# First attention of a two-layer decoder block: scores on four row quarters of the array

## The chip, the core and the metric

One core of a Trainium2 chip. The metric is device time of one execution in microseconds (us); lower is better. The engines are named as in the profile: PE is TensorE (matmuls; PEld its weight loads), DVE is VectorE, ACT is ScalarE, POOL is GpSimd, SP the queue that issues transfers.

## What is computed

Two layers, each an attention over a latent context and a feed-forward block, on x of 32 x 100 x 256. The change touches the attention of the first layer alone:

```python
x = x + tanh(g_xattn[0]) * _L0_xattn_ref(layernorm(x), ctx_512, Wq, Wkv_expand, Wout)

def _L0_xattn_ref(q, latent_kv, Wq, Wkv_expand, Wout):      # 16 heads of 16
    qp = q @ Wq.T
    k, v = jnp.split(latent_kv @ Wkv_expand.T, 2, axis=-1)
    scores = einsum('bhqd,bhkd->bhqk', qh, kh) / sqrt(16)
    scores = where(causal, scores, finfo.min)
    out = einsum('bhqk,bhkd->bhqd', softmax(scores), vh)
    return out @ Wout.T
```

The mask is causal, so of the 1444 context rows only the first 100 matter to 100 query rows, and the kernel loads only these.

## The kernel before

The program runs one phase after another: loading, first attention, experts, second attention, second feed-forward. `phase_l0_attention` (line 79) is the phase that changes. It takes the 32 batch elements ("batches" below) in 8 groups of 4, and its engines each run a list of instructions in the order in which the code is written, with semaphores between them; there is no scheduler. A group first makes its dense products on PE (`dense`, nine steps: normalised rows and latents transposed, queries at line 360, keys at 366, values at 372), which DVE copies out (`evacuate`). Queries and keys then lie with the 256 head dimensions on partitions, in two chunks k of 128, so 8 heads of 16 partitions in each chunk; `qt` and `kt` hold 100 columns a batch.

For each batch, 16 heads go in four quarters q of 4 heads, each with a bank of the accumulation memory, `s_ps[:, q]`, 4 x 100 columns:

- DVE (`block_keys`, line 222): the keys of a batch, repeated 8 times along the columns and multiplied by a selector, so that each head's columns are zero outside its own 16 partitions. That is `kbd`, 128 x 800 for each chunk.
- PE (`scores`): a bfloat16 matmul writes the mask into the bank (383), then one float32 matmul of 128 rows and 400 columns adds the scores of four heads (384). The float32 matmul stands in the trace as two.
- DVE (`differences`): maximum over each head's keys (234) and scores minus maximum (238). ACT takes the exponential (323).
- PE transposes the four heads' probabilities (425), ACT copies them (316), PE multiplies them with the values, which carry a column of ones (414). With four quarters done DVE divides by the sums (245, 247), PE transposes the result (394) and projects it (400), and DVE adds it to x (252).

The order around the change is written out by hand in PE's `group`: scores of batch 0, and then, in batch b and quarter q, first the scores of batch b + 1 and quarter q, then the transposes of batch b and quarter q, then the values of quarter q - 1. In the last batch of a group the dense steps of the next group stand between. DVE's list is in step: in batch b and quarter q it handles the differences of batch b + 1 and quarter q, and between them `block_keys`, `add_x` and the next group's row statistics. The bank of a quarter is free for new scores when DVE has taken the differences of the batch before; that is the wait on `diff_ready`:

```python
pe.wait_ge(diff_ready, PRIMED + n - NQ + 1 if b > 0 else it * G * NQ)
o = s_ps[0:S, q, 0:4 * S]
pe.matmul(o, identb[0:S, 0:S], mask[:]..., start=True, stop=False)
mm = pe.matmul(o, qt[:, q // 2, b * S:(b + 1) * S], kbd[b % 2][:, q // 2, 4 * (q % 2):4 * (q % 2) + 4, :]..., start=False, stop=True)
```

Of the kernel before, what the change touches and what calls it, by code (L numbers as in the profile page):

```python
# [9 lines left out]
ALU = mybir.AluOpType  # L10
# [3 lines left out]
B, S, D = 32, 100, 256  # L14
LK, DL = 1444, 64
G = 4
NG = B // G
T = G * S
KT = D // 128
H = 16  # L20
HD = D // H
# [13 lines left out]
PRIMED = 1  # L35
# [43 lines left out]
def phase_l0_attention(nc, outer, sem, io, m):  # L79

    NQ = 4
    counters = []
    with ExitStack() as ctx:
        sb = lambda n, s, d=F32: ctx.enter_context(nc.sbuf_tensor(n, s, d))
# [11 lines left out]
        mask_raw = sb("a_mask_raw", [S, S])  # L96
        mask = sb("a_mask", [S, 4, S], BF16)
        identb = sb("a_identb", [128, 128], BF16)
        headsel_raw, headsel = sb("a_headsel_raw", [128, 8]), sb("a_headsel", [128, 8, S])
        latg = sb("a_latg", [S, G + 1, DL])  # L100
        stats, mv, ve, rstd = sb("a_stats", [S, G, 6]), sb("a_mv", [S, G, 2]), sb("a_ve", [S, G]), sb("a_rstd", [S, G])
        xn = sb("a_xn", [S, G, D])
# [1 line left out]
        latt = [sb(f"a_latt{i}", [DL, T], F32R) for i in range(2)]  # L104
        qt = sb("a_qt", [128, KT, T])
        kt = sb("a_kt", [128, KT, T])
        kbd = [sb(f"a_kbd{i}", [128, KT, 8, S]) for i in range(2)]
        va = sb("a_va", [S, G, H, HD + 1])
        mx = sb("a_mx", [S, NQ, 4])
        diff = sb("a_diff", [S, NQ, 4, S])  # L110
# [1 line left out]
        pt = sb("a_pt", [S, 2, 4, S])  # L112
# [3 lines left out]
        s_ps = ps("a_s_ps", [128, 4, 512])  # L116
        p_ps = ps("a_p_ps", [128, 2, 512])
        o_ps = ps("a_o_ps", [128, 512])
        f_ps = ps("a_f_ps", [128, 512])
        w_loaded, w_ready = sem("a_w_loaded"), count("a_w_ready")  # L120
# [3 lines left out]
        kbd_ready, split_hi, latg_ready = count("a_kbd_ready"), count("a_split_hi"), count("a_latg_ready")  # L124
# [10 lines left out]
        with nc.Block() as block:  # L135
# [36 lines left out]
            def _(v):  # L172
# [7 lines left out]
                v.memset(va[:, :, :, HD], 1.0).then_inc(w_ready, 1)  # L180
                v.memset(latg[:, G, :], 0.0).then_inc(w_ready, 1)
                v.tensor_copy(identb[:], m.ident[:]).then_inc(w_ready, 1)
                v.tensor_copy(headsel[:], headsel_raw[:].unsqueeze(2).broadcast_to((128, 8, S))).then_inc(w_ready, 1)
                v.wait_ge(w_ready, PRIMED + NW)
                def row_stats(it):
                    xg = lambda j: m.x[:, bass.ds((it * G + j) * D, D)]
# [29 lines left out]
                def block_keys(it, b):  # L216

                    if b >= 2:

                        v.wait_ge(s_ready, PRIMED + (it * G + b - 1) * NQ)  # L220
                    for k in range(KT):
                        ins = v.tensor_tensor(kbd[b % 2][:, k], headsel[:],
                                              kt[:, k, b * S:(b + 1) * S].unsqueeze(1).broadcast_to((128, 8, S)),
                                              ALU.mult)
                    ins.then_inc(kbd_ready, 1)

                def group(it, more):
                    xg = lambda j: m.x[:, bass.ds((it * G + j) * D, D)]
# [103 lines left out]
            def _(pe):  # L332
# [41 lines left out]
                    mm.then_inc(dense_mm, 1)  # L374

                def group(it, more):
                    def scores(b, q):
                        n = it * G * NQ + b * NQ + q
                        pe.wait_ge(kbd_ready, PRIMED + it * G + b + 1)

                        pe.wait_ge(diff_ready, PRIMED + n - NQ + 1 if b > 0 else it * G * NQ)
                        o = s_ps[0:S, q, 0:4 * S]
                        pe.matmul(o, identb[0:S, 0:S], mask[:].rearrange("p h k -> p (h k)"), start=True, stop=False)
                        mm = pe.matmul(o, qt[:, q // 2, b * S:(b + 1) * S],
                                       kbd[b % 2][:, q // 2, 4 * (q % 2):4 * (q % 2) + 4, :].rearrange("p h k -> p (h k)"),
                                       start=False, stop=True)
                        mm.then_inc(s_ready, 1)

                    def turn_out(b):
                        nb = it * G + b  # L390
                        pe.wait_ge(cn_ready, PRIMED + nb + 1)
                        pe.wait_ge(x_added, PRIMED + nb)
                        for k in range(KT):
                            mm = pe.transpose(f_ps[:, 256 + k * S:256 + (k + 1) * S], cn[:, k * 128:(k + 1) * 128], m.ident[0:S, 0:S])
                        mm.then_inc(ct_ready, 1)

                    def project_out(b):
                        pe.wait_ge(ct_copied, PRIMED + it * G + b + 1)
                        for k in range(KT):
                            mm = pe.matmul(f_ps[0:S, 0:D], ct[:, k, :], wo[:, k, :], start=(k == 0), stop=(k == KT - 1))  # L400
                        mm.then_inc(f_ready, 1)
                    pe.wait_ge(dense_out, PRIMED + (it + 1) * ND)
                    for q in range(NQ):
                        scores(0, q)
                    for b in range(G):
                        nb = it * G + b

                        def probs_value(q):
                            n = nb * NQ + q
                            pe.wait_ge(pt_copied, PRIMED + n + 1)  # L410
                            if q == 0:
                                pe.wait_ge(cn_ready, PRIMED + nb)
                            for h in range(4):
                                mm = pe.matmul(o_ps[0:S, (4 * q + h) * (HD + 1):(4 * q + h + 1) * (HD + 1)],
                                               pt[:, q % 2, h, :], va[:, b, 4 * q + h, :], start=True, stop=True)
                            mm.then_inc(pv_done, 1)
                        for q in range(NQ):
                            n = nb * NQ + q
                            if b + 1 < G:
                                scores(b + 1, q)  # L420
                            pe.wait_ge(prob_ready, PRIMED + n + 1)
                            if b * NQ + q >= 2:
                                pe.wait_ge(pt_copied, PRIMED + n - 1)
                            for h in range(4):
                                mm = pe.transpose(p_ps[0:S, q % 2, h * S:(h + 1) * S], prob[:, q, h, :], m.ident[0:S, 0:S])
                            mm.then_inc(pt_ready, 1)
                            if q == 0 and b > 0:
                                turn_out(b - 1)
                            if q == 2 and b > 0:
                                project_out(b - 1)  # L430
                            if b == G - 1 and more:
                                for k in BESIDE_MM[q]:
                                    dense(it + 1, k)
                            if q > 0:
                                probs_value(q - 1)
                        probs_value(NQ - 1)
                    if more:
                        for k in range(7, ND):
                            dense(it + 1, k)
                    turn_out(G - 1)  # L440
                    project_out(G - 1)
# [1423 lines left out]
def constants():  # L1865
    import numpy as np
    c = {}
    c["ident"] = np.eye(128, dtype=np.float32)
    q, k = np.arange(S)[:, None], np.arange(S)[None, :]
    c["causal"] = np.where(k <= q, 0.0, -1e30).astype(np.float32)  # L1870
    c["headsel"] = (np.arange(128)[:, None] // HD == np.arange(8)[None, :]).astype(np.float32)
    row_expert = np.arange(E * I) // I
    rows = np.zeros((40, E * I), np.float32)
    for e in range(E):
# [50 lines left out]
```

## Time and profile before

| what | value |
|---|---|
| time, median of 3 runs | 3704.04 us (3701.6 to 3706.81) |
| time of the profiled execution | 3701.05 us |
| its span, first to last instruction | 3699.2 us |
| PE busy | 3111.9 us, 84% of the span |
| DVE busy | 2443.3 us, 66% |
| mean granted clock of PE | 0.924 |
| first attention, from its first score matmul to its end | 41.7 to 445.7 us |

The profile is of one execution. Its rows give start and length of instructions or groups of them; lengths of PE's matmuls contain a modelled end that lies under the next one, so what one occupies is read from start to start. PEclk is the granted share of PE's clock: 1.00 is 2.4 GHz, 0.50 is 1.2 GHz.

### The profile page before, as it was taken

What the parts mean: (1) busy time and instruction counts of PE and PEld (TensorE: products, weight loads), DVE (VectorE), ACT (ScalarE), POOL (GpSimd) and SP (SyncE); (2) the same over time, 40 slices, a digit from 0 to 9 for tenths busy, and PEclk for the clock granted to TensorE, in tenths of its full rate; (3) what the DMA queues carried; (4) which work ended last, traced back from release to release, by engine and by line L of the source; (5) the groups of instructions that cost most, each with busy time, mean ns of one, the idle gap of its engine ahead of it and who ended that gap; (6) DMA issues with size and microseconds to landing.
All of it is one profiled execution on the core that took longest, in us unless ns stands there. A gap on an engine that the chain in (4) does not pass through costs nothing. (4 is left out here: it accounts for less than half of the span.)

```text
span 3699.2 us, 56177 instructions
## 1 busy us (share of the span) xinstructions
PE 3111.9 (84%) x16648; PEld 2139.2 (58%) x16656; DVE 2443.3 (66%) x3485; ACT 1282.0 (35%) x2714; POOL 1581.2 (43%) x1062
## 2 busy tenths in 40 slices
PE   6999799997789988989888998898988899888244
PEld 5777688886555555555555555555555555555123
DVE  5777744443666676676676666667667667764787
ACT  1333222221243333333333333333332343333356
POOL 0000022221455545545555554554555555554467
PEclk9899799998899999999999999999999999999566
DMA  3000000002100000000000000000000000000200
GB/s 100 0 0 0 23 20 0 0 0 76 27 18 16 16 13 18 16 6 23 18 10 19 16 16 13 18 16 6 23 19 9 19 16 16 7 14 11 78 13 23
DMA packets 129494, 70.05 MB, mean 19 GB/s; under 512 B 83497, under 2 KB 123785, under 8 KB 129155
## 3 DMA queue, kind: packets, MB, share of 16 engines
q1 hardware_dynamic: 129218, 66.79, 7.2%
q8 instruction: 123, 2.02, 0.2%
q14 instruction: 153, 1.25, 0.1%
HBM read 56.30 MB, written 10.04 MB: 18 GB/s over the span
## 5 line engine op out<-in xcount | busy, mean ns | idle before, releaser
L1079 POOL TENSOR_TENSOR c_psum<-c_p 120x800 f32<-120x800 f32 (+1 forms) x384 | 758.8, 1976 | 873.4 <-ACT c_p L1291 492.9
L1136 DVE TENSOR_REDUCE c_mneg<-c_m_ps 128x1 fp32r<-128x1452 f32 (+1 forms) x448 | 746.5, 1666 | 440.2 <-PE c_m_ps L1330 433.6
L1291 ACT ACTIVATE c_p<-c_s_ps 120x400 f32<-120x400 f32 (+1 forms) x1536 | 650.0, 510 | 957.2 <-PE c_s_ps L1413 886.2
L1426 PE MATMUL c_o_ps<-c_p,c_val 120*64 120x400 f32 (+1 forms) x3072 | 609.8, 519 | 0.0
L1412 PE MATMUL c_s_ps<-c_q,c_k 128*120 128x400 f32 (+1 forms) x1536 | 556.4, 362 | 37.1 <-DMA c_q<-c_mneg 28.9
L1413 PE MATMUL c_s_ps<-c_q,c_k 65*120 65x400 f32 (+1 forms) x1536 | 539.6, 351 | 0.0
L1330 PE MATMUL c_m_ps<-c_k,c_q 128*128 128x484 f32 (+1 forms) x1344 | 408.4, 412 | 95.6 <-DVE c_mneg L1136 94.7
L1330 PEld LDWEIGHTS c_m_ps<-c_k,c_q 128*128 128x128 f32 (+1 forms) x1344 | 211.2, 179 | 329.9 <-DVE c_mneg L1136 215.2
L1070 POOL TENSOR_TENSOR c_rot<-c_rc,c_rs 96x400 f32<-96x400 f32 x256 | 261.3, 1040 | 281.0 <-DVE c_rs L1178 279.5
L1412 PEld LDWEIGHTS c_s_ps<-c_q,c_k 128*120 128x120 f32 (+1 forms) x1536 | 287.2, 187 | 128.4 <-issue 108.1
L1426 PEld LDWEIGHTS c_o_ps<-c_p,c_val 120*64 120x64 f32 (+1 forms) x3072 | 189.4, 138 | 271.1 <-issue 154.0
L1159 DVE TENSOR_TENSOR c_acc<-c_acc,c_psum 120x800 f32<-120x800 f32 x256 | 317.7, 1241 | 23.5 <-POOL c_psum L1079 21.1
L1353 PE MATMUL c_s_ps<-c_xt,l_a 128*96 128x400 f32 x1536 | 307.1, 351 | 1.8 <-DVE c_xt L1124 1.8
L1413 PEld LDWEIGHTS c_s_ps<-c_q,c_k 65*120 65x120 f32 (+1 forms) x1536 | 287.6, 187 | 12.7
L1353 PEld LDWEIGHTS c_s_ps<-c_xt,l_a 128*96 128x96 f32 x1536 | 248.0, 164 | 58.9 <-issue 11.6
L1247 ACT ACTIVATE c_q<-c_o_ps 64x400 fp32r<-64x400 f32 x256 | 127.7, 499 | 398.4 <-PE c_o_ps L1368 393.7
L522 POOL TENSOR_TENSOR b_act_lo<-b_act,b_act_hi 128x400 fp32r<-128x400 f32 x88 | 91.6, 1045 | 322.6 <-ACT b_act_hi L664 322.6
L709 PE MATMUL b_gu_ps<-b_xt,l_a 128*128 128x400 f32 x1056 | 213.9, 354 | 11.2 <-DVE b_gated L556 11.2
L709 PEld LDWEIGHTS b_gu_ps<-b_xt,l_a 128*128 128x128 f32 x1056 | 193.4, 193 | 18.1 <-DVE b_gated L556 18.0
L1343 PE MATMUL c_m_ps<-l_cvo,c_ct 128*100 128x256 f32 x512 | 132.6, 418 | 52.3 <-DVE c_ct L1144 45.7
L1178 DVE TENSOR_TENSOR c_rc<-c_s_ps,c_qcos 96x400 f32<-96x400 f32 x256 | 144.5, 565 | 33.2 <-PE c_s_ps L1353 27.5
L1144 DVE TENSOR_TENSOR c_ct<-c_onum,c_rdb 128x400 f32<-128x400 f32 x64 | 111.7, 1745 | 61.1 <-DMA c_rdb<-l_denominators 60.9
(218 smaller groups left out, 4159.7 us busy)
## 6 DMA issues: line engine op xcount, KB each, us to landing
c_rdb<-l_denominators SPq DMA_DIRECT2D x128, 100.0 KB, 2.7
c_kv<-in_ctx SPq DMA_DIRECT2D x32, 360.0 KB
c_q<-c_mneg SPq DMA_DIRECT2D x384, 0.5 KB, 1.9
c_den<-c_oden SPq DMA_DIRECT2D x256, 0.8 KB
x_rows<-in_x SPq DMA_DIRECT2D x4, 800.0 KB
x_spill<-x_rows SPq DMA_DIRECT2D x1, 3200.0 KB
c_xa<-x_spill SPq DMA_DIRECT2D x8, 400.0 KB
c_xr<-x_spill SPq DMA_DIRECT2D x32, 100.0 KB
```

Source lines behind the costliest of these rows:

```text
L709: mm = pe.matmul(gu_ps[:, t % 2, j, 0:T], w[wi][:, k, t * 128:(t + 1) * 128], xt[x][:, k, :], start=(i == 0 and k == 0), stop=(i == 2 and ...
L1070: g.tensor_tensor(rot[:, i % 4, a, :], rc[:, a, :], rs[:, a, :], ALU.add).then_inc(rot_ready, 1)
L1079: g.tensor_tensor(psum[0:k, u % 2, :], p[0:k, 2 * u % 4, :], p[0:k, (2 * u + 1) % 4, :], ALU.add).then_inc(psum_ready, 1)
L1136: v.tensor_reduce(mneg[0:n, c, t:t + 1], m_ps[0:n, :, 0:4 * KP], AX.XY, ALU.max, negate=True).then_inc(mneg_ready, 1)
L1159: v.tensor_tensor(acc[0:k, :], acc[0:k, :], psum[0:k, q % 2, :], ALU.add).then_inc(acc_ready, 1)
L1178: v.tensor_tensor(dst[:, a, :].rearrange("p (b s) -> p b s", b=G), wide_bank(i, half)[0:HALF, 0:T].rearrange("p (b s) -> p b s", b=G), tab ...
L1291: a.activation(p[0:k, w % 4, i * HALFQ:(i + 1) * HALFQ], s_ps[0:k, (2 * w + i) % 4, 0:HALFQ], ACT.Exp).then_inc(exp_ready, 1)
L1330: mm = pe.matmul(m_ps[0:n, k, 0:4 * KP], q1[:, j, c * CQS + t * 128:c * CQS + t * 128 + n], k1[j % 2][:, k * 4 * KP:(k + 1) * 4 * KP], sta ...
L1353: mm = pe.matmul(wide_bank(i, a)[0:HALF, 0:T], m.a[w][:, k, HEADS[i], a * HALF:(a + 1) * HALF], xt[x][:, k, :], start=(q == 0 and k == 0), ...
L1412: pe.matmul(o, k1[j % 2][:, r * KP:r * KP + k], q1[:, j, cols], start=True, stop=False)
L1413: mm = pe.matmul(o, k2[j % 2][:, r * KP:r * KP + k], q2[:, j, cols], start=False, stop=True)
L1426: mm = pe.matmul(o_ps[i * DL:(i + 1) * DL, 0:HALFQ], val[0:k, j % 2, r, :], p[0:k, w % 4, i * HALFQ:(i + 1) * HALFQ], start=(r == 0), stop ...
```

## The change

The 16 heads are grouped anew, and the scores of a batch are written as one block. Partitions 32q to 32q + 31 of each chunk hold two heads. Quarter q now takes these two heads of chunk 0 and the two of chunk 1 (table `QH`), so each of its matmuls reads 32 partitions alone: two heads, 200 columns. `kbd` needs only two head slots a chunk (selector of 2 columns in place of 8, repeating every 32 partitions), made by one DVE instruction of 128 x 400. `scores(b)` writes four masks into four banks, then eight matmuls, chunk by chunk and in each chunk quarter by quarter, on rows 0, 32, 64 and 96 in turn. It stands once ahead of a batch's loop over quarters, no longer inside it.

```diff
+    QH = [(2 * q, 2 * q + 1, H // 2 + 2 * q, H // 2 + 2 * q + 1) for q in range(NQ)]
...
-        kbd = [sb(f"a_kbd{i}", [128, KT, 8, S]) for i in range(2)]
+        kbd = [sb(f"a_kbd{i}", [128, KT, 2, S]) for i in range(2)]
...
-                    for k in range(KT):
-                        ins = v.tensor_tensor(kbd[b % 2][:, k], headsel[:],
-                                              kt[:, k, b * S:(b + 1) * S].unsqueeze(1).broadcast_to((128, 8, S)),
-                                              ALU.mult)
-                    ins.then_inc(kbd_ready, 1)
+                    v.tensor_tensor(kbd[b % 2][:], headsel[:].unsqueeze(1).broadcast_to((128, KT, 2, S)),
+                                    kt[:, :, b * S:(b + 1) * S].unsqueeze(2).broadcast_to((128, KT, 2, S)), ALU.mult).then_inc(kbd_ready, 1)
...
-                    def scores(b, q):
-                        n = it * G * NQ + b * NQ + q
+                    def scores(b):
+                        n = it * G * NQ + b * NQ
                         pe.wait_ge(kbd_ready, PRIMED + it * G + b + 1)
-
-                        pe.wait_ge(diff_ready, PRIMED + n - NQ + 1 if b > 0 else it * G * NQ)
-                        o = s_ps[0:S, q, 0:4 * S]
-                        pe.matmul(o, identb[0:S, 0:S], mask[:].rearrange("p h k -> p (h k)"), start=True, stop=False)
-                        mm = pe.matmul(o, qt[:, q // 2, b * S:(b + 1) * S],
-                                       kbd[b % 2][:, q // 2, 4 * (q % 2):4 * (q % 2) + 4, :].rearrange("p h k -> p (h k)"),
-                                       start=False, stop=True)
-                        mm.then_inc(s_ready, 1)
+                        for q in range(NQ):
+                            pe.wait_ge(diff_ready, PRIMED + n - NQ + q + 1 if b > 0 else it * G * NQ)
+                            pe.matmul(s_ps[0:S, q, 0:4 * S], identb[0:S, 0:S], mask[:].rearrange("p h k -> p (h k)"), start=True, stop=True)
+                        for k in range(KT):
+                            for q in range(NQ):
+                                rows = slice(32 * q, 32 * q + 32)
+                                mm = pe.matmul(s_ps[0:S, q, 2 * k * S:2 * (k + 1) * S], qt[rows, k, b * S:(b + 1) * S],
+                                               kbd[b % 2][rows, k].rearrange("p h k -> p (h k)"), start=False, stop=True, skip_group_check=True)
+                                if k == KT - 1:
+                                    mm.then_inc(s_ready, 1)
...
-                    for q in range(NQ):
-                        scores(0, q)
+                    scores(0)
...
-                                mm = pe.matmul(o_ps[0:S, (4 * q + h) * (HD + 1):(4 * q + h + 1) * (HD + 1)],
-                                               pt[:, q % 2, h, :], va[:, b, 4 * q + h, :], start=True, stop=True)
+                                mm = pe.matmul(o_ps[0:S, QH[q][h] * (HD + 1):(QH[q][h] + 1) * (HD + 1)],
+                                               pt[:, q % 2, h, :], va[:, b, QH[q][h], :], start=True, stop=True)
                             mm.then_inc(pv_done, 1)
+                        if b + 1 < G:
+                            scores(b + 1)
                         for q in range(NQ):
                             n = nb * NQ + q
-                            if b + 1 < G:
-                                scores(b + 1, q)
```

PE, batch 0 of a group, behind the scores of batch 0, as it stands before (each REGISTER_ALU forms the value that the next instruction waits for):

```order
L383 MATMUL a_s_ps<-a_mask,a_identb 100x400
L384 MATMUL a_s_ps<-a_kbd,a_qt 100x400
L425 MATMUL a_p_ps<-ident,a_prob 100x100 x4
L381 REGISTER_ALU
L383 MATMUL a_s_ps<-a_mask,a_identb 100x400
L384 MATMUL a_s_ps<-a_kbd,a_qt 100x400
L425 MATMUL a_p_ps<-ident,a_prob 100x100 x4
L412 REGISTER_ALU
L414 MATMUL a_o_ps<-a_va,a_pt 100x17 x4
```

One mask and one score matmul of batch 1 stand ahead of each four transposes of batch 0. The same place in the changed kernel:

```order
L380 MATMUL a_s_ps<-a_mask,a_identb 100x400
L379 REGISTER_ALU
L380 MATMUL a_s_ps<-a_mask,a_identb 100x400
L384 MATMUL a_s_ps<-a_kbd,a_qt 100x200 x8
L424 MATMUL a_p_ps<-ident,a_prob 100x100 x8
L411 REGISTER_ALU
L413 MATMUL a_o_ps<-a_va,a_pt 100x17 x4
```

These are the last two of the four masks; all four, each with its own wait on `diff_ready`, and the eight score matmuls of batch 1 have moved ahead of the first transpose of batch 0.

DVE at the start of a group, before:

```order
L222 TENSOR_TENSOR a_kbd<-a_headsel,a_kt 128x800 x2
L232 ISA
L234 TENSOR_REDUCE a_mx<-a_s_ps 100x4
L238 TENSOR_TENSOR a_diff<-a_s_ps,a_mx 100x400
L232 REGISTER_ALU
```

and in the changed kernel:

```order
L222 TENSOR_TENSOR a_kbd<-a_headsel,a_kt 128x400
L230 ISA
L232 TENSOR_REDUCE a_mx<-a_s_ps 100x4
L236 TENSOR_TENSOR a_diff<-a_s_ps,a_mx 100x400
L230 REGISTER_ALU
```

Here only the key selection differs: one instruction of half the columns for two; DVE's order stays.

## Rows read from the trace of the kernel before

**Rows 1.** The page, part 1: busy time of each engine over the span.
```profile
PE 3111.9 (84%) x16648; PEld 2139.2 (58%) x16656; DVE 2443.3 (66%) x3485; ACT 1282.0 (35%) x2714; POOL 1581.2 (43%) x1062
```
**Rows 2.** Stretches of the stage: length, busy time (instructions) by engine, PEclk, DMA share, GB/s.
```profile
41.70:445.70 404.00, 373.94 (x2406) 291.57 (x2406) 307.56 (x607) 131.27 (x288) 9.45 (x13) 0.87 0.01 4
128.00:134.00 6.00, 6.00 (x24) 5.42 (x24) 1.60 (x4) 0.50 (x1) 0.00 (x0) 0.50 0.00 0
135.00:138.00 3.00, 3.00 (x26) 2.58 (x24) 1.49 (x3) 0.50 (x1) 0.00 (x0) 1.00 0.00 0
139.00:147.00 8.00, 7.57 (x26) 5.46 (x26) 4.08 (x10) 0.34 (x1) 0.40 (x1) 0.50 0.00 0
149.00:178.00 29.00, 27.64 (x207) 21.17 (x206) 26.00 (x57) 13.53 (x30) 1.01 (x1) 1.00 0.00 0
428.80:435.00 6.20, 6.20 (x34) 5.66 (x33) 3.29 (x3) 1.72 (x4) 0.00 (x0) 0.50 0.00 0
```
**Rows 3.** Timeline of PE, one quarter at 2.4 GHz: start us, length us, instruction.
```profile
204.54 0.35 PE L383 MATMUL a_s_ps<-a_mask,a_identb 100*100 100x400 bf16 x1
204.73 0.84 PE L384 MATMUL a_s_ps<-a_kbd,a_qt 128*100 128x400 f32 x2
205.41 0.51 PE L425 MATMUL a_p_ps<-ident,a_prob 100*100 100x100 f32 x4
205.75 0.80 PE L414 MATMUL a_o_ps<-a_va,a_pt 100*100 100x17 f32 x8
206.40 0.35 PE L383 MATMUL a_s_ps<-a_mask,a_identb 100*100 100x400 bf16 x1
```
**Rows 4.** Timeline of PE in the stretches at 1.2 GHz.
```profile
127.75 2.18 PE L360 MATMUL a_s_ps<-a_xt,a_wq 128*128 128x400 f32 x6 [1.34 <-DVE a_xt L205]
129.73 1.40 PE L414 MATMUL a_o_ps<-a_va,a_pt 100*100 100x17 f32 x8
130.97 0.89 PE L425 MATMUL a_p_ps<-ident,a_prob 100*100 100x100 f32 x4
131.65 1.92 PE L400 MATMUL a_f_ps<-l_cvo,a_ct 128*100 128x256 f32 x4
...
139.69 2.88 PE L372 MATMUL a_s_ps<-a_wv,a_latt 64*100 64x256 f32 x12
142.50 0.59 PE L394 MATMUL a_f_ps<-ident,a_cn 100*128 100x100 f32 x2
143.52 2.03 PE L400 MATMUL a_f_ps<-l_cvo,a_ct 128*100 128x256 f32 x4 [0.43 <-ACT a_ct L309]
145.34 0.54 PE L383 MATMUL a_s_ps<-a_mask,a_identb 100*100 100x400 bf16 x1
145.67 1.54 PE L384 MATMUL a_s_ps<-a_kbd,a_qt 128*100 128x400 f32 x2
147.01 0.54 PE L383 MATMUL a_s_ps<-a_mask,a_identb 100*100 100x400 bf16 x1
```
**Rows 5.** Key matmuls on 64 rows: timeline of PE, and line 366 (ns min/median/max).
```profile
84.79 0.53 PE L425 MATMUL a_p_ps<-ident,a_prob 100*100 100x100 f32 x4
85.25 1.36 PE L366 MATMUL a_s_ps<-a_latt,a_wk 64*128 64x400 f32 x6
...
L366 PE MATMUL a_s_ps<-a_latt,a_wk x48: 338/342/450, 36.2 to 390.1; 64*128 64x400 f32 x48
```
**Rows 6.** Timeline of DVE: reduces of a group's start, and a key selection.
```profile
199.73 0.57 DVE L234 TENSOR_REDUCE a_mx<-a_s_ps 100x4 f32<-100x400 f32 x1
...
200.82 0.56 DVE L234 TENSOR_REDUCE a_mx<-a_s_ps 100x4 f32<-100x400 f32 x1
...
206.27 1.88 DVE L222 TENSOR_TENSOR a_kbd<-a_headsel,a_kt 128x800 f32<-128x800 f32 x2
208.07 0.57 DVE L234 TENSOR_REDUCE a_mx<-a_s_ps 100x4 f32<-100x400 f32 x1
```
**Rows 7.** Timeline of PE: the first transposes of the same group.
```profile
202.36 0.51 PE L425 MATMUL a_p_ps<-ident,a_prob 100*100 100x100 f32 x4
```

More of the change, by code:

```diff
@@ L98, in phase_l0_attention @@
         identb = sb("a_identb", [128, 128], BF16)
-        headsel_raw, headsel = sb("a_headsel_raw", [128, 8]), sb("a_headsel", [128, 8, S])
+        headsel_raw, headsel = sb("a_headsel_raw", [128, 2]), sb("a_headsel", [128, 2, S])
         latg = sb("a_latg", [S, G + 1, DL])
@@ L182, in _ @@
                 v.tensor_copy(identb[:], m.ident[:]).then_inc(w_ready, 1)
-                v.tensor_copy(headsel[:], headsel_raw[:].unsqueeze(2).broadcast_to((128, 8, S))).then_inc(w_ready, 1)
+                v.tensor_copy(headsel[:], headsel_raw[:].unsqueeze(2).broadcast_to((128, 2, S))).then_inc(w_ready, 1)
                 v.wait_ge(w_ready, PRIMED + NW)
@@ L1870, in constants @@
     c["causal"] = np.where(k <= q, 0.0, -1e30).astype(np.float32)
-    c["headsel"] = (np.arange(128)[:, None] // HD == np.arange(8)[None, :]).astype(np.float32)
+    c["headsel"] = (np.arange(128)[:, None] // HD % 2 == np.arange(2)[None, :]).astype(np.float32)
     row_expert = np.arange(E * I) // I
```

## The prediction

> **What bounds the kernel now.** I read the page first, then the stage, then one quarter of a batch, then the clock. The page names TensorE (PE) as the busiest engine, 84% of the span [rows 1]. The stage that the change touches runs from 41.7 to 445.7 us: 404 us for eight groups of four batches, 50.5 us a group; PE is busy for 374 us of it and VectorE (DVE) for 308 [rows 2]. So PE sets the pace, and DVE is not far behind. One quarter of a batch at 2.4 GHz takes 1.86 us on PE without a gap: mask 0.19, score pair 0.68, four transposes 0.34, probabilities times values 0.65 [rows 3]. The "x2" on the score matmul is one float32 matmul run as two passes over the same rows of the array.
>
> The third thing to read is the clock. In the whole stage it stands at 0.87, so at 1.2 GHz for about a quarter of the time [rows 2]. What the engine did before it moved: from 149 to 178 us, with score pairs all along, it stands at 1.00. From 128 to 134 us PE is busy without a break (query weights, transposes, values) and the clock is 0.50. It rises to 1.00 for 135 to 138, right behind the query-weight matmuls, which are 128 rows high and 400 columns long; in that stretch PE is again busy without a break, with key matmuls 64 rows high and short value products, and then the clock falls and stays at 0.50 from 139 to 147, until masks and score pairs come. From 428.8 to 435, after the last score pair, PE is fully busy at 0.50 [rows 2, 4]. So "busy" on the page did not go with the high clock. What went with it, in these stretches or just ahead of them, were long matmuls of full height, and in a regular batch those are above all the four score pairs.
>
> **The change, part by part.** All is summed against the profiled execution's own 3701.05 us (span 3699.2, 1.85 around it); the median of the runs shown, 3704.04, is 3 us above it.
>
> *Score matmuls.* Removed: four pairs a batch, 4 x 0.68 = 2.72 us [rows 3]. Added: eight matmuls of 200 columns on 32 rows, each two passes, and each half a pair long, 0.34 us. No row of this trace has matmuls on different rows side by side, so the bounds are one after the other, 8 x 0.34 = 2.72 us (nothing gained), and four quarters abreast, 0.68 us plus the tail. I take 1.5 us: the two passes of one matmul need the same rows, so with starts in program order, as in every row here, only the second pass of one quarter and the first of the next can run together, 8 x 0.17, and 0.17 behind it. Sixteen weight loads instead of eight cost nothing more: the eight loads and short matmuls of a value product pass in 0.65 us [rows 3], so sixteen need 1.3 us, beside the 1.5.
>
> *Switching the array's height.* The key matmuls on 64 rows behind full-height transposes start at 85.25, where 84.79 + 0.34 = 85.13 was free, 0.12 late, and the longest of them takes 450 ns against a median of 342, 0.11 more [rows 5]; with another 0.12 for the way back I take 0.35 us for a switch there and back, once a batch, 32 x 0.35 = 11 us (lower end 0.11 x 32 = 4).
>
> *Masks.* The same four a batch, 0.19 us each: nothing. *Selected keys on DVE.* Two instructions of 800 elements, 1.80 us from start to start, become one of 400; a reduce over 400 takes 0.57 [rows 6]. That frees 1.3 us a batch on an engine that PE hides; I count zero. If DVE became the bound it would be worth up to 32 x 1.3 = 42 us. The values' head order changes only addresses. The smaller load and copy of the selector lie in the start, under the input load: below 1 us.
>
> *The moved order.* Today the transposes of batch 0 start at 202.36, 2.6 us after the first reduce at 199.73, when one quarter's difference is through [rows 6, 7]. Now scores of batch 1 stand ahead of them as a block, and its last mask needs all four differences of batch 0, at 1.09 us each [rows 6]. PE then waits at each group's start for 4 x 1.09 less three or four masks, 3.6 us; behind it are queued the transposes, and behind those ACT's copies. That is 8 x 3.6 = 29 us. In the other batches the differences are finished beside transposes and value products; a wait of about 1 us where DVE also has the next group's statistics I leave in the range.
>
> *At an unchanged clock* this gives -32 x (2.72 - 1.5) + 11 + 29 = +1 us: 3702.
>
> *The clock.* The score matmuls now cover 32 rows instead of 128 and a shorter time, as the key matmuls on 64 rows cover half. After their stretch the clock fell [rows 2], and now nothing but masks and the output projection is both long and nearly full in height. I forecast 1.2 GHz for most of the stage. Its price from rows at 0.50 [rows 4], for one batch: masks 4 x 0.33 (145.34 to 145.67) = 1.3; scores, half a pair of 1.34 (145.67 to 147.01) is 0.67, two abreast 0.335, 8 x 0.335 + 0.335 = 3.0; transposes 4 x 0.68 (130.97 to 131.65) = 2.7; value products 4 x 1.24 (129.73 to 130.97) = 5.0; projection 1.8 (143.52 to 145.34); turning the output 0.4 (of 0.59 with its tail); switches 0.35. Sum 14.6 us, four batches 58.4. The dense work of a group: twelve transposes at 0.17 (a quarter of 0.68), 2.0; query weights 2 x 1.98 (127.75 to 129.73), 4.0; keys, 1.36 at the high clock [rows 5], 2.6; values 2.8 (139.69 to 142.50): 11.4. Waits: the group's start 3.4, before the query weights 1.34, before the projection 0.43: 5.2. Together 75.0 us a group. In between the clock will rise behind the query weights as it did at 135, for some 3 us and at times twice; what runs there would have taken double, so I take off 5: 70.0. Against 50.5 that is +19.5 a group, 8 x 19.5 = +156 us, 3857. With three high stretches a group it is 65, 3817; with none 75, 3897.
>
> **Rivals.** *1. A busy PE keeps its clock.* Then the sum above holds, 3702, within the bound of what a measurement of this kernel can tell from no change, 0.2% or 7.4 us. For it: PE stays busy for most of the stage. Against it: 128 to 134 and 428.8 to 435, busy to the last tenth and at 0.50 [rows 2]. The Trainium skill, "TensorE: Matmul & The Clock Gate", section "Why this matters for your kernels", has it that a TensorE kept busy without long gaps between bursts keeps the high clock; by that rule the time is this rival's 3702, and these two stretches disagree with it.
>
> *2. The quarters run fully abreast and the clock holds* (the side of faster). Mechanism: the array takes one pass of each quarter at a time, so a batch's scores take 0.68 + 0.17 = 0.85 us instead of 1.5, 32 x 0.65 = 21 us less: 3681. It decides as soon as scores fall below about 1.3 us a batch and the stage's clock is 0.87 or better. Against it: two passes on the same rows, and the clock. The same page, section "Measured speedup vs the span model", measured 3.07 times for four row quarters; a batch's scores would by that be an estimated 0.89 us. No run here shows it. At the low clock this case comes to 32 x 1.3 = 42 us less than the forecast, 3815, and belongs to it.
>
> *3. The quarters do not overlap at all, at the low clock*: 8 x 0.67 = 5.4 instead of 3.0 us a batch, 32 x 2.4 = 77 us more: 3934. For it: nothing in this trace shows two matmuls side by side.
>
> *4. The clock falls only behind the new wait at the group's start.* Then one stretch of 3 to 6 us a group at half speed costs 1.7 to 3.4 us: 3702 + 14 to 27, 3716 to 3729. For it: long waits of PE are the other thing that stands ahead of falls (1.34 us idle just before 127.75 [rows 4]). Against it: falls that no wait precedes.
>
> **How the numbers follow.** Forecast (mostly low clock, quarters two or four abreast) 0.66; rival 1, 0.06; rival 2, 0.10; rival 3, 0.08; rival 4, 0.10. The predicted time is the forecast's 3857; its own range is 3815 to 3897. The range 3700 to 3900 takes in rivals 1 and 4 and leaves out 2 and 3, together 0.18. Slower is forecast, 3 and 4: 0.84; same is 1: 0.06; faster is 2: 0.10.
>
> **What would show it.** Right: clock of the stage near 0.55, a group of 65 to 75 us, value products of 1.24 us a quarter nearly everywhere, key selection at 0.57 us, PE idle about 3.5 us at a group's start with single masks in it. The eight score matmuls of a batch in 1.5 us (3.0 at the low clock) confirm two abreast; 0.9 or 2.7 (1.7 or 5.4) refute it. The prediction is wrong if the stage's clock stays at 0.8 or more: then the time is near 3700 and its sign hangs on the width of the overlap.

## The result, and the profile after

The changed kernel takes 3788.28 us (median of 4 runs, 3778.96 to 3798.03) against 3705.43 us for the kernel before on the same chip: a ratio of 1.0227, 95% interval 1.0205 to 1.025. It is slower, by 83 us. The profiled execution took 3778.96 us, its span is 3777.2.

The page, part 1:

```profile
PE 3171.6 (84%) x16904; PEld 2207.9 (58%) x16912; DVE 2403.6 (64%) x3453; ACT 1278.2 (34%) x2714; POOL 1582.5 (42%) x1062
```

The key selection on DVE, by line (count, ns min/median/max, first and last start, shape):

```profile
L222 DVE TENSOR_TENSOR a_kbd<-a_headsel,a_kt x32: 562/565/576, 41.0 to 489.2; 128x400 f32<-128x400 f32 x32
```

PE's share is the same 84% as in [rows 1], though its score matmuls became shorter. The stage, and four stretches in it (columns as in [rows 2]):

```profile
41.70:519.30 477.60, 433.34 (x2662) 357.59 (x2662) 269.98 (x576) 126.47 (x288) 9.46 (x13) 0.63 0.01 4
106.50:111.00 4.50, 2.01 (x20) 0.96 (x19) 3.95 (x8) 1.07 (x2) 0.00 (x0) 0.87 0.00 0
112.50:125.00 12.50, 12.50 (x85) 10.47 (x84) 5.48 (x11) 3.60 (x8) 0.00 (x0) 0.50 0.00 0
127.00:132.80 5.80, 5.01 (x49) 4.34 (x47) 5.51 (x17) 3.02 (x7) 1.01 (x1) 1.00 0.00 0
134.00:145.00 11.00, 10.95 (x62) 9.84 (x58) 6.77 (x15) 3.85 (x10) 0.00 (x0) 0.50 0.00 0
```

The stage grew from 404.0 to 477.6 us, 73.6 of the 78.0 us by which the span grew (3699.2 to 3777.2). Its clock fell from 0.87 [rows 2] to 0.63. Between two levels, 0.63 means that 2 x (1 - 0.63) = 74% of the stage, 353 us, ran at 1.2 GHz; before it was 26%, 105 us. From 112.5 to 125 us PE is busy without any break and stands at 0.50 throughout.

What happens there, in PE's timeline (start us, length us, instruction, in brackets the idle time before it):

```profile
106.56 0.94 PE L384 MATMUL a_s_ps<-a_kbd,a_qt 32*100 32x200 f32 x16
108.75 0.37 PE L380 MATMUL a_s_ps<-a_mask,a_identb 100*100 100x400 bf16 x1 [1.25 <-DVE a_diff L236]
109.84 0.57 PE L380 MATMUL a_s_ps<-a_mask,a_identb 100*100 100x400 bf16 x1 [0.71 <-DVE a_diff L236]
110.93 0.57 PE L380 MATMUL a_s_ps<-a_mask,a_identb 100*100 100x400 bf16 x1 [0.52 <-DVE a_diff L236]
112.02 0.57 PE L380 MATMUL a_s_ps<-a_mask,a_identb 100*100 100x400 bf16 x1 [0.51 <-DVE a_diff L236]
112.52 1.67 PE L384 MATMUL a_s_ps<-a_kbd,a_qt 32*100 32x200 f32 x16
114.12 1.57 PE L424 MATMUL a_p_ps<-ident,a_prob 100*100 100x100 f32 x8
115.69 1.51 PE L413 MATMUL a_o_ps<-a_va,a_pt 100*100 100x17 f32 x8
...
197.22 0.37 PE L380 MATMUL a_s_ps<-a_mask,a_identb 100*100 100x400 bf16 x1 [0.60 <-DVE a_diff L236]
197.52 0.94 PE L384 MATMUL a_s_ps<-a_kbd,a_qt 32*100 32x200 f32 x16
198.39 0.55 PE L424 MATMUL a_p_ps<-ident,a_prob 100*100 100x100 f32 x4
```

This shows both things that the prediction priced. The four masks of batch 1 at a group's start come singly, each waiting for DVE. And the sixteen passes of a batch's scores take 198.39 - 197.52 = 0.87 us at 2.4 GHz where four pairs took 2.72 [rows 3], and 114.12 - 112.52 = 1.60 us at 1.2 GHz. So the matmuls themselves are three times as fast as before, and the stage is longer all the same. The 0.87 from 106.5 to 111 us says where the clock fell: at 109.8, inside this wait. By the trace's clock records it fell inside the wait at the start in seven of the eight groups (in the first it was low already).

PE's waits in the stage (us in total, times, longest), after, and then before:

```profile
PE a_s_ps L380 <- DVE a_diff L236: 28.3, 37, 1.3
PE a_f_ps L394 <- DVE a_cn L245: 8.8, 5, 6.1
PE a_s_ps L358 <- DVE a_xt L206: 2.5, 7, 0.4
```

```profile
PE a_f_ps L394 <- DVE a_cn L247: 18.8, 23, 6.1
PE a_s_ps L360 <- DVE a_xt L205: 6.5, 7, 1.3
```

The new wait on the differences is 28.3 us, but 10.0 and 4.0 us of other waits have gone: PE comes to them later. The account is then, with low-clock time counted at half: before, 404 - 105/2 = 351 us of full-speed time; after, 477.6 - 353/2 = 301. The change takes 50 us away, and the clock takes 353/2 - 105/2 = 124 us, which makes the +74. (It is rough, since a wait for DVE does not shrink with PE's clock. Counting only the time in which PE was busy at 1.2 GHz, 92.9 us before and 335.5 after by the trace's clock records, the clock takes 121 us, the waits 14, and the work itself is 62 us less.)

### The profile page after: what moved, and what is told of

Its sections match the earlier page's. It is cut to its first block and busy times, and to the rows that moved or that the text cites. A ratio compares the mean times of both kernels' runs of the same rounds, so it can differ in the third digit from the quotient of the medians.

```text
span 3777.2 us, 56624 instructions
## 1 busy us (share of the span) xinstructions
PE 3171.6 (84%) x16904; PEld 2207.9 (58%) x16912; DVE 2403.6 (64%) x3453; ACT 1278.2 (34%) x2714; POOL 1582.5 (42%) x1062
## 5 line engine op out<-in xcount | busy, mean ns | idle before, releaser
L1135 DVE TENSOR_REDUCE c_mneg<-c_m_ps 128x1 fp32r<-128x1452 f32 (+1 forms) x448 | 746.4, 1666 | 439.3 <-PE c_m_ps L1329 432.8
L413 PEld LDWEIGHTS a_o_ps<-a_va,a_pt 100*100 100x100 f32 x1024 | 151.9, 239 | 10.1 <-issue 4.7
```

Source lines behind the costliest of these rows:

```text
L413: mm = pe.matmul(o_ps[0:S, QH[q][h] * (HD + 1):(QH[q][h] + 1) * (HD + 1)], pt[:, q % 2, h, :], va[:, b, QH[q][h], :], start=True, stop=True)
L1135: v.tensor_reduce(mneg[0:n, c, t:t + 1], m_ps[0:n, :, 0:4 * KP], AX.XY, ALU.max, negate=True).then_inc(mneg_ready, 1)
```

## Experiments

Two theories stood at the start. A: score matmuls of 32 rows no longer hold the clock. B: it is the idle time at the group's start, which the moved order brings, that lets it fall. All runs of the kernel before beside them had medians from 3696.8 to 3704.7 us. Stage and clock are those of each run's one profiled execution.

| run | median us | ratio to before (95%) | stage us | clock of stage |
|---|---|---|---|---|
| before (profile) | 3704.0 | | 404.0 | 0.87 |
| changed | 3788.3 | 1.0227 (1.0205 to 1.025) | 477.6 | 0.63 |
| e1_order_alone | 3737.2 | 1.0096 (1.0058 to 1.0134) | 432.8 | 0.85 |
| e2_rows_alone | 3964.2 | 1.0694 (1.0662 to 1.0726) | 652.6 | 0.53 |
| e3_fill_every_batch | 3744.4 | 1.0115 (1.0083 to 1.0147) | 430.1 | 0.88 |
| e4_fill_start | 3751.4 | 1.0137 (1.0101 to 1.0173) | 453.1 | 0.69 |
| e5_late_block | 3834.8 | 1.036 (1.0321 to 1.0398) | 527.7 | 0.57 |
| e6_late_block_fill | 3864.0 | 1.0438 (1.0398 to 1.0478) | 571.1 | 0.72 |
| e7_late_block_half_fill | 3829.4 | 1.0353 (1.0301 to 1.0405) | 527.7 | 0.73 |
| e8_late_block_mask_twice | 3835.8 | 1.0365 (1.0326 to 1.0404) | 526.2 | 0.66 |
| e9_fill_mid | 3749.6 | 1.0138 (1.0093 to 1.0182) | 451.7 | 0.71 |
| e10_half_fill | 3787.4 | 1.0226 (1.0188 to 1.0265) | 485.3 | 0.70 |
| e11_mask_twice | 3800.5 | 1.026 (1.0216 to 1.0303) | 503.5 | 0.63 |
| e12_fill_odd | 3720.9 | 1.005 (1.0033 to 1.0067) | 427.5 | 0.79 |

### The two halves of the change apart

Order alone: the block of four masks and scores, each score matmul on 128 rows and 400 columns as before, and the key selection as before too. The diffs here and below are against the changed kernel, shortened.

```diff
-                        for k in range(KT):
-                            for q in range(NQ):
-                                mm = pe.matmul(... qt[rows, k, ...], kbd[b % 2][rows, k]...)
+                        for q in range(NQ):
+                            mm = pe.matmul(s_ps[0:S, q, 0:4 * S], qt[:, q // 2, ...], kbd[b % 2][:, q // 2, 4 * (q % 2):4 * (q % 2) + 4, :]...)
```

> The moved order alone: the score matmuls as before (128 rows, 400 columns, key selection of 800 columns), but the four masks and four score matmuls of a batch stand as one block ahead of the transposes, as in the changed kernel. Theory A (the 32-row score matmuls no longer keep PE's clock up): the granted clock of the first attention stays at 0.80 or more, PE waits some 3.5 us at each group's start, and the time is 3725 to 3765 us. Theory B (the wait at the group's start is what drops the clock): the clock of the stage falls to 0.70 or less as in the changed kernel, and the time is above 3790 us, since the scores are also four times as long.

Rows alone: 32-row score matmuls, in the order of the kernel before, one quarter's mask and four passes ahead of each four transposes.

```diff
-                    def scores(b):
+                    def scores(b, q):
...
-                        for k in range(KT):
-                            for q in range(NQ):
+                        rows = slice(32 * q, 32 * q + 32)
+                        for k in range(KT):
...
+                            if b + 1 < G:
+                                scores(b + 1, q)
```

> The 32-row score matmuls alone: key selection of 400 columns, two heads on 32 partitions, but the quarters in the order of the kernel before (mask and two score matmuls of one quarter of the next batch ahead of each four transposes), so no quarter runs beside another and PE has no wait at a group's start. Theory A: the clock of the stage falls to 0.55 to 0.65 and the time is 3830 to 3890 us. Theory B: the clock stays at 0.85 or more; only four switches of the array's height a batch are added, 32 x 4 x 0.35 = 45 us: 3735 to 3755 us.

The order alone costs 35 us and keeps 0.85. PE's wait on the differences in it:

```profile
PE a_s_ps L382 <- DVE a_diff L238: 15.2, 23, 0.7
```

That is half of the changed kernel's 28.3 us, so this run tests B with half of the idle time. The rows alone cost 262 us and bring 0.53. The whole stage and a stretch of the second, its longest waits of PE in the stage, and one quarter in its timeline:

```profile
40.80:693.40 652.60, 639.30 (x2662) 484.98 (x2662) 280.29 (x576) 129.63 (x288) 9.47 (x13) 0.53 0.01 5
60.00:690.00 630.00, 617.69 (x2590) 471.31 (x2590) 270.98 (x559) 125.86 (x280) 9.47 (x13) 0.53 0.00 0
```

```profile
PE a_f_ps L391 <- DVE a_cn L245: 6.1, 1, 6.1
PE a_f_ps L397 <- ACT a_ct L307: 3.4, 8, 0.4
```

```profile
300.50 0.55 PE L379 MATMUL a_s_ps<-a_mask,a_identb 100*100 100x400 bf16 x1
300.98 1.65 PE L382 MATMUL a_s_ps<-a_kbd,a_qt 32*100 32x200 f32 x4
302.56 0.91 PE L422 MATMUL a_p_ps<-ident,a_prob 100*100 100x100 f32 x4
```

There is no wait on the differences at all, PE is busy for 617.69 of 630 us, and the clock is at its low level nearly all the time. So the low clock does not need B's idle time, and rival 1 is refuted. It also parts two things that the prediction named together, 32 rows and a shorter time: here a quarter's mask and scores take longer than before, and the clock is lower still. What the wait adds in the changed kernel, where the clock falls inside it, is left to the next runs. The Trainium skill, "TensorE: Matmul & The Clock Gate", section "Why this matters for your kernels", advises to keep TensorE busy continuously for the high clock; the stretch from 60 to 690 us, busy for 98% and at 0.53, is the plainest disagreement in the case. The time lies 74 us above theory A's upper end. Of these, 50 are explained by a lone quarter, which overlaps with nothing: mask to first score 0.48 us and four passes with their way back 1.58, together 2.06, where mask and pair at 1.2 GHz took 1.67 before [rows 4]; 128 x 0.39 = 50 us.

### Putting full-height work back

A matmul whose result the mask overwrites, ahead of every mask (e3, the diff shown), and under `if b == 1:` ahead of the masks of batch 1 alone, inside the waits of a group's start (e4).

```diff
+                            pe.matmul(s_ps[0:S, q, 0:D], wo[:, 0, 0:S], wo[:, 0, :], start=True, stop=True)
                             pe.matmul(s_ps[0:S, q, 0:4 * S], identb[0:S, 0:S], mask[:]..., start=True, stop=True)
```

> The changed kernel with work added: ahead of every mask one float32 matmul of 128 rows and 256 columns on the output weights, written to the same bank and overwritten by the mask; the output is unchanged. That adds four times 0.43 us a batch at 2.4 GHz, 55 us in all. Theory A: the clock of the stage rises to 0.80 or more, and in spite of the added work the time falls below the changed kernel's 3788 us, to 3690 to 3740. Theory B: only the filler in the group's start wait helps; then this comes out some 30 to 50 us above e4.

> The changed kernel with the same added matmul, but only ahead of the four masks of batch 1 of each group, where PE waits for DVE anyway, so that the wait is filled with full-height work. Theory A: the clock of the stage stays between 0.60 and 0.70 and the time within 15 us of 3788. Theory B: the clock goes back to 0.85 and the time to 3690 to 3715 us.

The stage with the filling in every batch, and two instructions of it:

```profile
40.70:470.80 430.10, 385.21 (x2917) 306.35 (x2915) 268.70 (x575) 125.14 (x288) 9.45 (x13) 0.88 0.02 6
```

```profile
202.88 0.60 PE L380 MATMUL a_s_ps<-l_cvo 128*100 128x256 f32 x2
203.32 0.33 PE L381 MATMUL a_s_ps<-a_mask,a_identb 100*100 100x400 bf16 x1
```

Each filling takes 203.32 - 202.88 = 0.44 us, so 128 x 0.44 = 56 us of useless work were added, and the kernel became 44 us faster than the changed one; the clock is back at 0.88. This is theory A's strongest support: no operand or order of the changed kernel differs but for this work, and PE's idle time in the stage is the same (430.10 - 385.21 = 44.9 us against 477.60 - 433.34 = 44.3). The filling at the start alone also helped, by 37 us, more than A had allowed. Two readings were left: it fills idle time (then idle time is a second cause, called C below), or its amount helps wherever it stands. The same dose in batch 3, where PE hardly waits (3.4 of the 28.3 us), tells them apart.

```diff
+                            if b == 3:
+                                pe.matmul(s_ps[0:S, q, 0:D], wo[:, 0, 0:S], wo[:, 0, :], start=True, stop=True)
```

> The changed kernel with one matmul of full height (128 rows, 256 columns, two passes, 0.43 us at 2.4 GHz, overwritten by the mask) ahead of each of the four masks of batch 3 alone, where PE has hardly a wait: 4 a group, 32 in all, 14 us of work at 2.4 GHz, the same dose that at the group's start, inside the waits, gave a clock of 0.69 and 3751 us. Theory A (the amount of full-height work counts, wherever it stands): clock 0.67 to 0.73, 3745 to 3780 us. Theory C (what the filling did there was to fill idle time, and idle time is a second cause of falls): clock 0.60 to 0.65, 3790 to 3815 us, which is the changed kernel's time plus 14 to 28.

3749.6 us at 0.71, the same as at the start: C falls. The stages of e4 and e9 say the same, with 37.5 and 49.8 us of idle time against the changed kernel's 44.3:

```profile
41.00:494.10 453.10, 415.57 (x2726) 338.59 (x2726) 270.18 (x576) 126.21 (x288) 9.46 (x13) 0.69 0.01 5
```

```profile
40.30:492.00 451.70, 401.87 (x2726) 324.78 (x2726) 269.38 (x576) 125.72 (x288) 9.46 (x13) 0.71 0.02 6
```

PE's timeline and three stretches around one such place in e9:

```profile
122.40 0.65 PE L381 MATMUL a_s_ps<-l_cvo 128*100 128x256 f32 x2
122.89 0.34 PE L382 MATMUL a_s_ps<-a_mask,a_identb 100*100 100x400 bf16 x1
...
124.97 0.94 PE L386 MATMUL a_s_ps<-a_kbd,a_qt 32*100 32x200 f32 x16
```

```profile
103.60:117.00 13.40, 13.40 (x89) 11.10 (x89) 6.02 (x12) 3.60 (x8) 0.00 (x0) 0.50 0.00 0
118.00:132.00 14.00, 13.89 (x132) 11.87 (x130) 12.09 (x32) 6.81 (x17) 1.01 (x1) 1.00 0.00 0
134.00:144.00 10.00, 8.66 (x70) 7.82 (x68) 6.13 (x12) 1.93 (x4) 0.00 (x0) 1.00 0.00 0
```

The start of this group is untouched: it waits as in the changed kernel, then 13 us at 0.50. The clock rises just ahead of the filling, as in the changed kernel at 127; but there it fell again at the next block of scores (0.50 from 134), and here, with the filling, it holds through that block to 144.

### The same block, moved later

> The changed kernel with the block of batch b + 1's masks and scores moved later in PE's list: ahead of the transposes of quarter 3 in a group's batch 0, of quarter 2 in batch 1, of quarter 1 in batch 2 (in the change: ahead of quarter 0 in each). The work is the same; PE has batch 0's first transposes and value products to do while DVE finishes its differences, so the idle time at a group's start (about 3.5 us) should go. Theory A (score matmuls on 32 rows no longer hold the clock): clock of the stage stays at 0.55 to 0.68, and the time falls by no more than the 29 us of waits, 3755 to 3790 us. Theory B (the idle time at the group's start lets the clock fall): clock 0.80 or more, and the stage is that of before less 32 x (2.72 - 0.87) = 59 us for the scores, 3640 to 3690 us. Both at work, as the run with filling at the start alone suggested: clock 0.68 to 0.80, 3690 to 3755 us.

```diff
-                        if b + 1 < G:
-                            scores(b + 1)
                         for q in range(NQ):
                             n = nb * NQ + q
+                            if b + 1 < G and q == 3 - b:
+                                scores(b + 1)
```

With the same later block, the filling as in e3, half of it, and each mask written twice:

> The kernel with the later block, and with one more matmul of full height ahead of every mask (128 rows, 256 columns, two passes, 0.43 us at 2.4 GHz, its result overwritten by the mask): 16 a group, 128 x 0.43 = 55 us of added work. Theory A: clock of the stage 0.85 or more; against the run with this filling at the change's own place (3744 us) the waits go, up to 29 us, so 3710 to 3740 us. Theory B: the clock is that of the run without filling, and the time is its time plus 55 us or more.

> As the run with the later block and filling, but with 128 columns in place of 256: 128 x 0.22 = 28 us of added work. Theory A, if half of it still holds the clock: 0.85 or more, 3685 to 3715 us; if it doesn't, the clock lies between those of the two other runs with the later block, 3715 to 3760 us. Theory B: the time of the run without filling plus 28 us.

> The kernel with the later block, each mask written twice (a bfloat16 matmul of 100 rows and 400 columns, 0.17 to 0.19 us at 2.4 GHz), so 128 x 0.18 = 23 us of added work that changes no result. Theory A, if one bfloat16 pass counts as much as a float32 pass of the same length: like the half filling, clock and time within 0.05 and 20 us of that run. If bfloat16 does not count, the clock is that of the run without filling and the time that run's plus 23 to 45 us. Theory B: the time of the run without filling plus 23 us at its clock.

Of theory A's bounds e5 missed the upper by 45 us, e6 by 124 and e7 by 69; e8 came within 20 us of e7, as expected, but 0.07 below its clock. Theory B missed as well: it had 3640 to 3690 us for e5. The waits of PE in e5's stage, and the stages of e5 and e8:

```profile
PE a_f_ps L394 <- DVE a_cn L245: 38.4, 18, 6.1
PE a_p_ps L424 <- ACT a_prob L321: 17.5, 16, 1.8
```

```profile
40.20:567.90 527.70, 464.66 (x2662) 383.20 (x2662) 269.26 (x576) 131.72 (x288) 9.46 (x13) 0.57 0.01 5
```

```profile
41.00:567.20 526.20, 444.00 (x2790) 356.15 (x2790) 268.81 (x577) 131.62 (x288) 9.46 (x13) 0.66 0.02 6
```

The 28.3 us on the differences are gone, and 38.4 + 17.5 took their place. The 17.5 stand at the groups' starts, two waits in each: PE now waits there for ACT's exponentials. The 38.4 had not been followed: DVE's list divides by the sums (line 245) only behind the differences of the next batch. A later block makes these late, and PE's turn of the output, next in PE's own list, waits for the division, 18 times in the stage. Of the 50 us by which e5's stage is longer than the changed kernel's, 19 are idle time (527.70 - 464.66 = 63.0 against 44.3 us); the rest is busy time, at a lower clock. So the block's early place, wait included, is the cheaper one.

Between A and B, e5 decides little: the idle time at a group's start shrank, from 3.1 to 2.2 us, but did not go, and other waits had come. What the four runs show is that added work raised the clock here too, the doubled masks included (0.66 in e8 against 0.57 in e5), and that it gained no time clear of noise, since PE's idle time grew with it (82.2 us in e8, 101.5 in e6).

### How much work, and how spread

The changed kernel's own order, with half the filling (128 columns) at every mask; with each mask written twice; and with the full filling in batches 1 and 3.

```diff
+                            pe.matmul(s_ps[0:S, q, 0:128], wo[:, 0, 0:S], wo[:, 0, 0:128], start=True, stop=True)
...
+                            pe.matmul(s_ps[0:S, q, 0:4 * S], identb[0:S, 0:S], mask[:]..., start=True, stop=True)
...
+                            if b % 2 == 1:
+                                pe.matmul(s_ps[0:S, q, 0:D], wo[:, 0, 0:S], wo[:, 0, :], start=True, stop=True)
```

> The changed kernel, its order kept, with a full-height matmul of 128 columns (0.22 us at 2.4 GHz) ahead of every mask: 128 x 0.22 = 28 us of work, half of the run in which 256 columns gave a clock of 0.88 and 3744 us. Theory A: if half is enough, clock 0.80 or more and 3705 to 3740 us (3744 less up to 28, some of which the waits already hid); if not, clock 0.68 to 0.80 and 3735 to 3765 us. It would beat the kernel before only below 3695.

> The changed kernel, its order kept, each mask written twice (bfloat16, 100 rows, 400 columns): 128 x 0.18 = 23 us of work at 2.4 GHz. Theory A: a clock of 0.68 to 0.80, and 3740 to 3785 us. If a second mask does not help the clock: 0.63, and 3788 plus 15 to 46 us less what the group's start hides, 3795 to 3830 us.

> The changed kernel with the full-height filling (256 columns, 0.43 us at 2.4 GHz) ahead of the masks of batches 1 and 3: 64 x 0.43 = 28 us of work, half of it inside the waits of the group's start. It is the same amount as 128 columns ahead of every mask, which gave 3787 us, but in two blocks a group instead of four thinner ones. If only the amount counts (theory A as it stood): about 3787 us. If blocks of it hold the clock better than the same amount spread thin: below both single doses (3751 and 3750), 3715 to 3745 us, clock 0.75 to 0.86. It would beat the kernel before only below 3690.

The stages of e10, e11 and e12, and masks of e11:

```profile
40.90:526.20 485.30, 439.64 (x2918) 367.57 (x2918) 269.35 (x577) 125.15 (x288) 9.47 (x13) 0.70 0.01 5
```

```profile
41.10:544.60 503.50, 463.85 (x2790) 372.89 (x2790) 270.45 (x576) 125.89 (x288) 9.46 (x13) 0.63 0.01 4
```

```profile
122.25 0.55 PE L380 MATMUL a_s_ps<-a_mask,a_identb 100*100 100x400 bf16 x1
122.60 0.54 PE L381 MATMUL a_s_ps<-a_mask,a_identb 100*100 100x400 bf16 x1
...
124.27 0.54 PE L380 MATMUL a_s_ps<-a_mask,a_identb 100*100 100x400 bf16 x1
124.60 0.54 PE L381 MATMUL a_s_ps<-a_mask,a_identb 100*100 100x400 bf16 x1
```

```profile
43.10:470.60 427.50, 386.83 (x2790) 310.44 (x2790) 269.14 (x576) 125.48 (x288) 9.46 (x13) 0.79 0.01 4
```

Doubled masks left the clock at 0.63, and the time is 12 us up, which the two intervals do not tell from none: eight of them one behind the other still step at 0.33 to 0.35 us, the low clock (122.25 to 124.60). Float32 fillings of half length, 28 us of work where the second masks are 23, brought 0.70. So a mask did less here than a float32 matmul of full height of about the same length, and in the late block as well (0.66 in e8, 0.73 in e7). That it does nothing is not shown: in e8 it raised the clock, and two of e11's four executions stood at 0.897 and 0.898 over the whole program, where the changed kernel's stood at 0.887 to 0.893. Whether the mask's type, its 100 rows or its single pass is the reason, no run separates. Half the filling everywhere raised the clock, as A expected, but its own work took back what that gave: 3787.4 us, 22 above A's range. The same 28 us as full filling in two of four batches gave 67 us (3720.9). So "only the amount counts" falls too: eight full fillings a group held the clock for longer (0.79) than sixteen halves (0.70). Waits explain little of it: a half of e12's work and a quarter of e10's stand inside the start's wait, 7 us of difference. At 3720.9, e12 is the fastest version with the new scores, and still 0.33 to 0.67% slower than the kernel before. No version here beats it.

## Why the prediction was right or wrong

The direction and the mechanism were right: slower, by the clock, with the time inside the stated range of 3700 to 3900. The 3857 was 69 us too high, and 3788 lies below the 3815 to 3897 that the forecast gave itself: the wider range holds it only because it was drawn to take in rivals 1 and 4.

- **Scores, the term that was wrong.** "Only the second pass of one quarter and the first of the next can run together", 1.5 us (3.0 at the low clock). Measured: 0.87 and 1.60. By the prediction's own test that refutes two abreast and shows four. In the single records of the block at 197.52, four passes start within 20 ns (197.524 to 197.544) and the next four from 197.774; the records do not say which pass is which, but four starting together is not what the prediction's argument from program order allowed. Rival 2's 0.85 us had the right width. The Trainium skill, "TensorE: Matmul & The Clock Gate", section "Measured speedup vs the span model", gives 3.07 times for four row tiles, by which a batch's scores take an estimated 0.89 us; this trace agrees, 2.72 / 0.87 = 3.1 times. At the low clock the error is 32 x (3.0 - 1.6) = 45 us.
- **Clock.** Forecast near 0.55, measured 0.63. The prediction gave each group some 5 us of useful high stretches; (1 - 0.74) x 477.6 / 8 = 15.5 us a group stood at 2.4 GHz, part of them the idle time at its start (0.87 from 106.5 to 111). By the trace's clock records PE was busy for 12.2 of them, 7 more than forecast. A group took 59.7 us on average, against 70.0 predicted (65 to 75), so in the stage the forecast was 8 x 10.3 = 82 us too high. The scores make 45 of that and the high stretches 8 x 7 = 56, so the other terms together were some 20 us too low: the errors partly cancelled. With four abreast at the low clock the text itself came to 3815; that is 27 us off.
- **Wait at the group's start.** Forecast 8 x 3.6 = 29 us. Of the 28.3 us in 37 waits, 32 waits stand at the starts and make 24.9, 3.1 a group; the other five, 3.4 us, stand at a last mask of batch 3 (197.22 is one). Not forecast: 14 us of other waits went in return.
- **Switching the array's height.** Forecast 0.35 us a batch. From the last mask to the scores 0.30 us (197.22 to 197.52) where a mask takes 0.19 [rows 3], 0.11 more; the block takes 0.87 where four steps of 0.17 would be 0.68, 0.19 more, the way back among it. About 0.3, as forecast.
- **Key selection.** Forecast 0.57 us, measured 0.565; DVE's busy time in the stage fell by 37.6 us (307.56 to 269.98), 1.17 a batch for the 1.3 forecast. Counted as zero because PE hides it; e1, which keeps the long selection, shows no new wait that would contradict this, but no run tried the short selection by itself.
- **Rivals.** Rival 1 is refuted by e2, and by the changed kernel itself from 112.5 to 125 us. Rival 2 was right on the overlap and wrong on the clock; at full speed the change would have been worth the 50 us of the account above. Rival 3 is what e2 met with its lone quarters: four passes in 1.58 us at the low clock, no better than the pair's 1.34. Rival 4, the order's wait alone, is only partly measured by e1, which keeps the long scores and waits half as long: by that rival's terms 29 + 14 to 27 = 43 to 56 us more, measured 35, with a clock of 0.85 against 0.87. (Its 14 to 27 do not follow from its own 3 to 6 us at half speed, which cost 1.5 to 3 a group, 12 to 24.) Of the 28.8 us in e1's stage, 10.3 are idle time (432.80 - 392.45 = 40.4 against 30.1) and 18.5 busy time; the clock has its part in these, some 12 us by the account above (130 us at 1.2 GHz against 105). That the clock fell inside the start's wait in the changed kernel fits this rival; e2 shows that the fall comes without a wait too.

What stays open: which property of the full-height filling holds the clock (rows, type, passes); whether it is the 32 rows or the 200 columns of a pass that make the new scores do without it, since every run with the new scores has both; and why fewer full fillings do better than twice as many halves.

## What to carry to other kernels

Before packing small matmuls onto row quarters of TensorE, look at the granted clock of the stretch and at what else runs in it: if the matmuls to be packed are nearly the only long ones of full height, the packing can be three times as fast by itself and still lose more at half clock in everything around it. Test it with a matmul that does nothing useful; if added work makes the kernel faster and the granted clock rises with it, the clock is the bound. And before a block is moved to a place without a wait, follow the other engine's list past it to the next thing that engine owes.

## What the runs showed of the hardware

- PE busy for 98% of 630 us (617.69) at a granted clock of 0.53, with score matmuls on 32 rows and 200 columns; and 56 us of added full-height float32 work that brought 0.63 back to 0.88 and saved 44 us.
- Float32 matmuls on four row quarters run four abreast, both passes too: 16 passes of 200 columns in 0.87 us at 2.4 GHz, in four steps of four (start to start 0.25, 0.17 and 0.17 us in the records at 197.52), 3.1 times as fast as the four pairs. Passes of one quarter do not overlap: four take 1.58 us at 1.2 GHz, way back included.
- Doubled bfloat16 masks of 100 rows and 400 columns did less for the clock than half-length float32 fillings of 128 rows: 0.63 against 0.70 in the changed order (0.63 without either), 0.66 against 0.73 with the later block (0.57 without either).
